# An audio tower's attention and expert block: another order of the work at the head

## What is computed

```python
logits = xn @ sn - sigmoid(gates)
q = einsum('tc,ecd,te->td', x, q_proj, m)      # k and v likewise
final = einsum('td,edc,te->tc', attn_out, o_proj, m * routing_weights)
```

## Time and profile before

| | |
|---|---|
| median of 3 runs | 722.53 us (721.84 to 722.65) |
| the profiled execution, its own time | 721.31 us |
| its span, first to last instruction | 719.6 us |
| TensorE busy (matmul) | 708.3 us, 98% |
| VectorE busy | 586.8 us, 82% |
| ScalarE busy | 371.9 us, 52% |
| GpSimd busy | 405.5 us, 56% |
| granted TensorE clock, mean | 1.000 |
| chain that ended last | 94% TensorE, 2% VectorE, 2% GpSimd |

### The profile page before, as it was taken

One profiled execution on the slowest core, in us unless ns is written; L12 is line 12 of the kernel. 1 busy time (PEld: TensorE's weight loads), 2 busy tenths in 40 slices (PEclk: granted clock), 3 DMA queues, 4 the chain that ended last, 5 costly groups with the idle time before them and its releaser, 6 DMA issues.

```text
span 719.6 us, 18107 instructions
## 1 busy us (share of the span) xinstructions
PE 708.3 (98%) x5384; PEld 467.0 (65%) x5384; DVE 586.8 (82%) x1474; ACT 371.9 (52%) x797; POOL 405.5 (56%) x657
## 2 busy tenths in 40 slices
PE   7999999999999999999999999999999999999996
PEld 6888666575756666575756666575756666575653
DVE  6788888888879888887979888887988898886626
ACT  3877463553646354553646354453646355463345
POOL 6542325746566575746566575746566574653344
PEclk9999999999999999999999999999999999999999
DMA  8681120202020110202020020202011020201000
GB/s 216 140 219 46 60 56 2 71 9 63 14 55 21 11 65 0 70 7 62 14 51 25 8 65 3 62 14 62 14 30 47 0 70 7 62 17 53 15 15 29
DMA packets 31216, 33.29 MB, mean 46 GB/s; under 512 B 5202, under 2 KB 27090, under 8 KB 31186
## 3 DMA queue, kind: packets, MB, share of 16 engines
q1 hardware_dynamic: 30114, 32.31, 16.9%
q10 hardware_dynamic: 1072, 0.60, 0.3%
HBM read 26.65 MB, written 6.25 MB: 46 GB/s over the span
## 4 chain that ended last, share of the span: by engine, by line
PE 94%; DVE 2%; POOL 2%; issue 1%; ACT 0%; POOLq 0%; DVEq 0%
PE bank L1520 75%; PE bank L1583 7%; PE bank L1442 4%; PE bank L1502 3%; PE bank L1654 1%; PE bank L1431 1%; PE bank L1569 1%; PE bank L1632 1%; PE bank L1447 1%; PE bank L1594 0%; DVE xm L1139 0%; PE bank L1605 0%; PE bank L1597 0%; POOL xhl L566 0%; POOL exp_hl L493 0%
## 5 line engine op out<-in xcount | busy, mean ns | idle before, releaser
L1520 PE MATMUL bank<-xm,w_qkv 128*128 128x374 f16 x2304 | 415.7, 322 | 0.0
L1520 PEld LDWEIGHTS bank<-xm,w_qkv 128*128 128x128 f16 x2304 | 220.7, 98 | 139.5 <-DVE xm L1139 0.3
L806 ACT ACTIVATE region_c<-bank,out_w 128x256 f32<-128x256 f32 x180 | 84.8, 471 | 164.9 <-PE bank L1520 164.9
L1139 DVE TENSOR_TENSOR xm<-xT,mask_all 128x1496 f16<-128x1496 f16 x128 | 151.0, 1184 | 1.4 <-ACT h L688 1.4
L1520 PE MATMUL bank<-w_o,aoT 128*128 128x512 f16 x540 | 145.7, 379 | 0.1
L1060 DVE SCALAR_TENSOR_TENSOR h<-bank,out_w,h 128x256 f32 (+1 forms) x180 | 86.2, 479 | 45.2 <-ACT region_c L806 40.1
L598 POOL TENSOR_TENSOR region_c<-region_c 128x512 f32<-128x512 f32 x47 | 77.6, 1652 | 27.7 <-ACT region_c L806 23.0
L613 POOL TENSOR_TENSOR exp_hl<-exp,exp_hl 128x128 f16<-128x128 f32 (+2 forms) x48 | 38.8, 809 | 75.5 <-ACT exp_hl L783 75.5
L1520 PEld LDWEIGHTS bank<-w_o,aoT 128*128 128x128 f16 x540 | 50.2, 98 | 38.2 <-DVE h L1060 0.7
L1039 DVE TENSOR_SCALAR region_b<-h,moments,small 128x256 f32 (+1 forms) x96 | 48.8, 553 | 5.7 <-POOL small L519 5.7
L604 POOL TENSOR_TENSOR h<-region_c,h 128x256 f32 (+1 forms) x47 | 42.0, 894 | 16.0 <-POOL region_c L601 11.4
(11 more groups left out here) (183 smaller groups left out, 1058.0 us busy)
## 6 DMA issues: line engine op xcount, KB each, us to landing
mask_all<-d_mask SPq DMA_DIRECT2D x32, 384.0 KB, 3.8
h<-in_x_dram SPq DMA_DIRECT2D x16, 256.0 KB, 5.7
out_dram<-h SPq DMA_DIRECT2D x32, 128.0 KB
rnorm_row<-d_rnorm SPq DMA_DIRECT2D x16, 192.0 KB, 3.6
h<-in_x_dram SPq DMA_DIRECT2D x16, 112.0 KB, 5.9
out_dram<-h SPq DMA_DIRECT2D x16, 112.0 KB
xm<-in_L_ffn_q_proj_dram SPq DMA_DIRECT2D x2, 512.0 KB, 9.0
region_c<-in_L_ffn_k_proj_dram SPq DMA_DIRECT2D x2, 512.0 KB, 7.3
```

The lines of the kernel that those rows point to most:

```text
L806: a.activation(prod[:, prod_buf(n, t), q, :], pair_bank(n, p)[:, C:2 * C], ACT.Copy, scale=weights_out(n)[:, t, 2 * q + 1:2 * q + 2]).then ...
L1139: v.tensor_tensor(xm[:, e, :, 0:T], xT[1][:, :, :, 0:T].rearrange("p a c t -> p (a c) t"), mask_all[:, e, 0:T].unsqueeze(1).broadcast_to([ ...
L1520: last = t_.matmul(dst, left[lp], right[rp], start=(starts and k == 0), stop=(stops and k == 2), skip_group_check=True)
```

## The change

The order of the head is changed on all engines, and no arithmetic:

- 38 warm-up matmuls instead of 46.
- SyncE loads weight piece 1 and the tiles of batch 7 ahead of the norm's round trip of batch 0.
- GpSimd sets `ones` ahead of `pick`.
- The bias has a semaphore of its own, so that TensorE's readout transposes no longer wait for it; these now come ahead of `turn_in(0)`, and the readout product ahead of `turn_in(1)`.
- ScalarE and VectorE round the token weights ahead of the first batch's split.
- The product with `ones` moves behind the whole projection of batch 0, and the wait for the last constant (`s_consts` 2) to `turn_first(0)`.
- `weights_high(0)` comes two batches earlier, `weights_high(1)` takes its place; `weights_low(1)` and `weights_low(2)` move earlier.
- The exponential's table is loaded by a dummy operation, and the gates' exponential comes behind those of batch 0's cosines.
- `route(0)` is no longer interrupted by `split_low(11)`, which precedes it.
- In the last batches of the head and in the branch `early(m)`: `mask_tokens(0, 1)` comes behind `split_low(15)` and `norm_apply(1, 1)`, `low_2(1)` ahead of `mask_tokens(0, 3)`, the wait for the last GELU ahead of the norm of batch 2, `weights_low(3)` behind `turned_low_2`; on TensorE the logits come one unit later, and the two halves of `turn_first` have a unit between them.

```diff
--- before.py
+++ after.py
@@ -178,6 +178,7 @@
         s_read_loaded = sem("read_loaded")
+        s_bias_loaded = sem("bias_loaded")
         s_consts = sem("consts")
@@ -296,7 +297,7 @@
         SPLIT = LAST // 16 * 16
-        WARM = 46
+        WARM = 38
         ENDS = (0, 1, 4, B)
@@ -418,11 +419,11 @@
             load_tiles(6)
+            load_weights(1)
+            load_tiles(7)
             norms_out(0)
             norms_in(0)
-            load_tiles(7)
             load_tiles(8)
-            load_weights(1)
             load_tiles(9)
@@ -474,6 +475,7 @@
             g.tensor_copy(ident16[:, :], ident[:, :]).then_inc(s_consts, 1)
+            g.memset(ones[:, :], 1.0)
             g.memset(pick32[:, :], 0.0).then_inc(s_picked, 1)
@@ -482,7 +484,6 @@
             g.tensor_copy(pick[:, :, :].rearrange("p b o -> p (b o)"), pick32[:, :]).then_inc(s_picked, 1)
-            g.memset(ones[:, :], 1.0)
             g.memset(p_half[:, :], 0.5)
@@ -662,7 +663,7 @@
             load_token_weights(1, s_tok_read)
-            act.dma_start(read_bias[:, :], tok_b.partition_broadcast(RR)).then_inc(s_read_loaded, 16)
+            act.dma_start(read_bias[:, :], tok_b.partition_broadcast(RR)).then_inc(s_bias_loaded, 16)
             for c in range(NC):
@@ -875,34 +876,35 @@
-            split_in(0)
             act.wait_ge(s_tok_loaded, 16)
             a.activation(w_tok[:, 0, :, :], stage_tok[:, 0, :, :], ACT.Copy, scale=W_SCALE).then_inc(s_tokw_hi, 1)
+            split_in(0)
             split_in(1)
...
             split_in(3)
+            weights_high(0)
             gelu(2)
...
             split_in(5)
-            weights_high(0)
+            weights_high(1)
             gelu(4)
...
             gelu(5)
-            act.wait_ge(s_small_loaded, 16 * (NC + 1))
-            a.activation(gate_tmp[:, 1, :], gate_tmp[:, 0, :], ACT.Exp, scale=-1.0).then_inc(s_gate_exp, 1)
+            a.activation(unused[:, :], log_p[:, :], ACT.Exp)
             exp_cosines(0, (0, 1))
...
             exp_cosines(0, (2,))
+            act.wait_ge(s_small_loaded, 16 * (NC + 1))
+            a.activation(gate_tmp[:, 1, :], gate_tmp[:, 0, :], ACT.Exp, scale=-1.0).then_inc(s_gate_exp, 1)
             gelu(6)
...
             a.activation(w_sim[:, :, 0, :], stage_sim[:, 3, :, :], ACT.Copy).then_inc(s_sim_hi, 1)
-            weights_high(1)
             gelu(7)
@@ -975,7 +977,7 @@
                 dve.wait_ge(s_setup_pe, 2)
-                dve.wait_ge(s_read_loaded, 32)
+                dve.wait_ge(s_bias_loaded, 16)
                 v.tensor_tensor(read_row[:, :], bank[4][0:RR, 0:C], read_bias[:, :], ALU.add).then_inc(s_setup_dve, 1)
@@ -1078,7 +1080,7 @@
-            def route(b, between=None):
+            def route(b):
@@ -1111,8 +1113,6 @@
                                       ALU.mult))
-                if between is not None:
-                    between()
                 v.tensor_scalar(row3[:, 1, :], row3[:, 0, :], 0.0, None, ALU.is_equal)
@@ -1252,13 +1252,12 @@
                 if early(m):
-                    mask_tokens(m, 3)
-                    low_2(f)
-                    for e in range(4, E):
+                    for e in range(3, E):
                         mask_tokens(m, e)
-                    weights_low(2 * NC - 1)
                     dve.wait_ge(s_xm_ready, E * f)
                     turned_low_2(f)
+                    weights_low(2 * NC - 1)
+                    dve.wait_ge(s_h_ready, B)
                     norm_stats(0, g1)
@@ -1355,8 +1354,8 @@
             read_columns()
+            token_weights_low()
             split_low(0)
-            token_weights_low()
             readout_row()
@@ -1374,6 +1373,7 @@
             split_low(6)
+            weights_low(1)
             cosines(0, 0)
@@ -1390,14 +1390,14 @@
             low_2(0)
-            weights_low(1)
             split_low(10)
             turned_low_2(0)
+            split_low(11)
             dve.wait_ge(s_consts, 2)
-            route(0, lambda: split_low(11))
+            route(0)
+            weights_low(2)
             weight_max(0)
             split_low(12)
-            weights_low(2)
             cosines(1, 0)
@@ -1410,11 +1410,11 @@
             mask_tokens(0, 0)
-            mask_tokens(0, 1)
             split_low(15)
             norm_apply(1, 1)
+            mask_tokens(0, 1)
             mask_tokens(0, 2)
-            dve.wait_ge(s_h_ready, B)
+            low_2(1)
             pipeline(dve, step)
@@ -1464,29 +1464,23 @@
                 t_.matmul(bank[6][:, 0:P], ident16[:, :], ident16[:, :], start=True, stop=True)
-            turn_in(0)
-
-            pe.wait_ge(s_read_loaded, 32)
+            pe.wait_ge(s_read_loaded, 16)
             pe.wait_ge(s_pad_zeroed, 2)
...
             last.then_inc(s_setup_pe, 1)
-            turn_in(1)
+            turn_in(0)
             pe.wait_ge(s_tok_read, 16)
...
             last.then_inc(s_setup_pe, 1)
+            turn_in(1)
             pe.wait_ge(s_tokw_lo, 1)
...
             project_tile(0, NT - 1)
-            pe.wait_ge(s_setup_dve, 3)
-            pe.wait_ge(s_consts, 2)
-            for c in range(NC):
-                last = t_.matmul(bank[5][:, 0:E], ones[:, :], stage_sim[:, 1, c, :], start=(c == 0), stop=(c == NC - 1))
-            last.then_inc(s_setup_pe, 1)
             pe.wait_ge(s_setup_dve, 6)
@@ -1494,6 +1488,9 @@
             add_row(0, NT - 1)
+            for c in range(NC):
+                last = t_.matmul(bank[5][:, 0:E], ones[:, :], stage_sim[:, 1, c, :], start=(c == 0), stop=(c == NC - 1))
+            last.then_inc(s_setup_pe, 1)
@@ -1503,15 +1500,23 @@
-            def turn_first(b):
+            def turn_first_high(b):
...
                 turn_rows(0, b, 0, turn[0], s_turned1_hi)
+
+            def turn_first_low(b):
+
                 pe.wait_ge(s_lo1, b + 1)
                 turn_rows(0, b, 1, turn[1], s_turned1_lo)
+
+            def turn_first(b):
+
+                turn_first_high(b)
+                turn_first_low(b)
@@ -1707,13 +1712,15 @@
                     turn_rows(1, f, 1, turn[1], s_turned2_lo)
-                    M(*range(2, 6))
+                    M(*range(2, 7))
                     logits(f)
-                    M(*range(6, 12))
+                    M(*range(7, 13))
                     turn_mask(f)
-                    M(*range(12, 22))
-                    turn_first(g1)
-                    M(22, 23)
+                    M(*range(13, 22))
+                    turn_first_high(g1)
+                    M(22)
+                    turn_first_low(g1)
+                    M(23)
                     return
@@ -1812,6 +1819,7 @@
             project(4)
+            pe.wait_ge(s_consts, 2)
             turn_first(0)
```

## The result

The changed kernel takes 718.67 us (median of six runs, 718.22 to 719.97) against 722.7 for the kernel before (six runs, 721.84 to 723.02) on the same chip: ratio 0.9948, 95% interval [0.9939, 0.9958]. It is faster, by 0.52%, and the forecast of 718.3 was 0.4 us too low. The profiled execution took 719.55, its span is 717.8.

What follows compares the result with a forecast made beforehand. TensorE was taken as the bound, always busy in the loop, so only its waits in the head could gain. The terms sum to 4.24 us, taking the median from 722.53 to 718.3 us, range 716.9 to 720.6.

Steps and rivals of the forecast that it cites:

- start: Opening of the head: pick product at 11.05 instead of 12.80, ones-product moved behind the batch: 1.47 us gained.
- piece 0 and the third GELU: Head, third GELU: ScalarE waits 0.6 for piece 0, first half ends 19.07, TensorE needs it at 19.03: -0.04 us.
- transposes behind routing: Head, transposes at 52.64: they no longer wait for a split placed in the middle of routing: 0.59 us.
- attention of batch 1: Head, at 62.54: 0.11 us kept of a possible 0.74, as piece 2's rounding slows GpSimd's mask steps.
- a split ahead of a mask product: Head, TensorE's gap at 71.04: moving a split ahead of one mask product gains 0.17 us.
- turned low rows of batch 1: Loop's first step: the gap from unit 1's end at 75.74 to the transposes at 75.98 goes, 0.24 us.
- first step's logits: Loop's first step: the gap from four units' end at 80.13 to the logits at 81.06 goes, 0.93 us.
- turned low rows of batch 2: End of the head: the wait from 97.06 to 97.54 goes, as a unit lies between the halves, 0.48 us.
- Rival (a): Head: GpSimd is not held up by piece 2's rounding, 0.63 us more gain, 717.6 us; chance 0.10.
- (c): Only the start's and the first step's gaps are real, new waits eat the rest: 721.1 to 724 us; chance 0.07.
- (d): Sync queue serves piece 0 with loads put behind it; it lands 6.0 late, holding the third GELU: 724.3 us; chance 0.03.
- (b): Head: piece 0 or the norm's round trip late, or the opening at 1.2 GHz: 719 to 721 us; chance 0.18.

Runs made afterwards that it cites:

- u1_split_between: Changed kernel with the split of batch 11 in the middle of routing again: 719.25 us, ratio 0.996 to the kernel before.
- u2_old_step: Changed kernel with VectorE's and TensorE's old order around the loop's first step: 719.5 us, ratio 0.9965 to the kernel before.
- u3_turn_joined: Changed kernel with both halves of batch 2's turned rows together, no unit between: 718.81 us, ratio 0.9958 to the kernel before.
- r1_after_again: The changed kernel run again, nothing edited: 717.66 us against 721.26 for the kernel before, ratio 0.9949.
- r2_row_first: Changed kernel with VectorE doing the readout row ahead of the square of the gate weights: 717.65 us, ratio 0.9949 to the kernel before.
- x1_pool_waits: r2_row_first, with GpSimd zeroing the two exponential tiles only after the readout row is split: 717.87 us, ratio 0.9932 to the kernel before.
- u5_ones_back: Changed kernel with the ones-product ahead of the pick product again, with its wait for GpSimd's constants: 720.58 us, ratio 0.997 to the kernel before.
- x2_piece_later: x1_pool_waits, with ScalarE's rounding of weight piece 0 behind the third GELU: 718.01 us, ratio 0.9935 to the kernel before.
- r3_max_later: Changed kernel with split_low(12) ahead of weight_max(0) on VectorE: 717.07 us, ratio 0.9943 to the kernel before.
- b2_all: x2_piece_later plus r3_max_later's edit and GpSimd's loop wait for the first mask product: 715.86 us, ratio 0.9907 to the kernel before.
- u4_warm_16: Changed kernel with 16 warm-up matmuls instead of 38: 718.41 us, ratio 0.9951 to the kernel before.

## Why the prediction was right, and where its steps were not

The sum was 4.24, the head gave 3.67 by the same steps. By these the profiled execution was to become 717.1; without long turns it took 717.65. That the median came within 0.4 of the forecast is luck in part: the medians differ by 4.03, more than the head's 3.66 can give, while where the kernel before is steady they differ by 3.60.

| step | forecast | measured | |
|---|---|---|---|
| start | 1.47 | 1.18 | mis-sized |
| piece 0 and the third GELU | -0.04 | 0 | right; ScalarE waits 0.28 and not 0.6, as the start gained 0.3 less |
| logits of batch 0 | 0.29 | 0.22 | nearly |
| transposes behind routing | 0.59 | 0.59 | right (u1_split_between: 0.71) |
| attention of batch 1 | 0.11 | 0.01 | size off, mechanism right |
| a split ahead of a mask product | 0.17 | 0 | wrong |
| turned low rows of batch 1 | 0.24 | 0.24 | right |
| first step's logits | 0.93 | 0.95 | right (with the row below, u2_old_step: 1.2) |
| turned low rows of batch 2 | 0.48 | 0.48 | right, half of it by the unit between (u3_turn_joined) |

**The start.** The step that was mis-sized is "then 0.1 and the old chain of 1.26 ... so 10.98". I took three durations of before as the operations' own. The second of them is a wait in disguise: it ends at 10.88 whether it begins at 10.51 (before), 10.29 (after), 10.02 (r1_after_again) or 8.36 (r2_row_first), because GpSimd's memsets of the exponential tiles hold it, and x1_pool_waits frees it (0.29). The chain could not move by 0.34 as I had it; it ended at 11.32 as before. The same sentence's other bound, a start at 8.4, would have given nothing either (r2_row_first). The whole 1.18 hangs on the move of the ones-product (u5_ones_back). Two slips of the sum are small: 1.31 and 0.17 make 1.48, and 9.60 + 0.1 + 1.26 makes 10.96.

**The clock.** I worked out a rise at 5.88 from one execution and called the case's own run evidence for the next. It rose between 6.6 and 7.8 in the two executions of the changed kernel, at about 5.0 in r2_row_first and x2_piece_later (the spacing of the warm-up falls from 0.107 to 0.056 there), near 8.1 in x1_pool_waits. The changed kernel paid nothing, since the hold on VectorE hid up to 1.18 us of it, but this was luck in my sum: without the hold the clock's moment is worth 0.78 of the start (x1_pool_waits against x2_piece_later). The Trainium skill (TensorE: Matmul & The Clock Gate, Part 1) says that the moment of the rise varies from run to run; the traces agree, with the same 38 matmuls in 4.24 and in 3.58 us.

**Rival (a)**, GpSimd not held by the rounding of piece 2, is refuted: its first mask step took 1.04. I had kept 0.11 of 0.74; 0.01 was had, and r3_max_later gets 0.62 of the rest back. Here I had read the hold in the earlier trace rows and used it. It is the same mechanism, seen from the other engine, that I missed at the start.

**The 0.17** was no gap of VectorE's making. In the changed kernel ScalarE's and TensorE's timelines have

```profile
68.48 0.60 ACT L686 ACTIVATE h<-bank 128x512 f32<-128x512 f32 x1 [1.04 <-PE bank L1447]
...
69.22 0.82 PE L1442 MATMUL bank<-w_tok,xinT 128*128 128x256 f16 x6
```

The projection starts 0.14 after the GELU's first part has read its bank (69.08), and before it was 0.14 too (70.47 + 0.60, then 71.21). VectorE's split, done at 70.93 before and at 68.10 after, shortens nothing there by being ready earlier. I had read the gap's length and not what ended it.

**"The loop hands on whatever shift it gets"** is true to 0.01 where the race goes the same way in every turn (the 13 turns behind the marker sum to 529.31 in r1_after_again and to 529.32 before) and is not a law: a turn in which a late mask lets GpSimd go first costs 0.55 to 0.76 more. Rivals (c) and (d) did not come about; the issue of piece 1 and of the tile load behind piece 0 did not delay it (9.3 again, and 8.8 to 9.5 in the other runs). Of (b) the low clock did come (the warm-up stood at it to its end), but the hold on VectorE hid it.

**The signs.** Two of the signs that I had named for being wrong appeared, though the forecast held: the warm-up spacing stayed at 0.107 to its end, and the shift shrank inside the loop. The first cost nothing, and the second was the race, so neither told what I had meant by it. Of the signs for being right, the marker stands at 97.07 and not near 96.5.

What stays open: I have one trace of the kernel before, and it has no long turn. That its medians of 722.4 and 722.46 in the later groups, against 721.26 in the first, come from such turns is argued only. Its times speak for it: the sixteen of the last group lie in four clusters (721.31 to 721.38, 721.82 to 721.96, 722.46 to 722.62, 723.01 to 723.26), 0.5 to 0.6 apart, about what one long turn costs. Whether zeroing on another engine than GpSimd would beat b2_all was not tried.

## What to carry to other kernels

- A duration read from a trace is not yet an operation's cost. Compare it with the same form elsewhere in the trace before it goes into a sum, and ask what the other engines ran beside it; an operation that always ends at the same moment is waiting.
- Work without a deadline (zeroing constants, a rounding that is needed later) can be on the critical path through a neighbour that it holds. One wait on a semaphore, which put it behind the urgent operation, was worth 0.26 to 1.04 us here at the pick product, by the clock's moment (on top of r2_row_first, which alone gave nothing).
- Where two engines race for the first start in each turn of a loop, fix the order by a wait. It cost nothing here in the turns that went well, and took the loss out of the others, not by ending the hold but by moving it to an operation that has time.

## What the runs showed of the hardware that I had not expected

- Some operations of VectorE and GpSimd hold each other, both ways, and the one that starts first keeps its speed. VectorE's scaling of a 48x256 tile: 0.28 to 0.29 alone, 2.52 beside the memsets. Its mask product: 0.97 first, 2.37 second. GpSimd's subtraction of the low rows: 1.61 first, 2.31 second; its mask step 1.04 beside a rounding of 1.22 and 0.24 without. VectorE's split, which reads PSUM (line 963), is not touched: it took 1.02 from 8.09, under the memsets of 7.27 to 10.61, and 1.02 from 7.89 in b2_all, where GpSimd was idle. The Trainium skill (GPSIMD Engine Reference, 1. Specifications) has the two sharing their SBUF interfaces, with contention for VectorE instructions in a 2-port mode or with two SBUF inputs. The traces agree as far as the operations named above go. In one point the Trainium skill and the measurement differ, and the measurement decides: not every instruction with two SBUF inputs is held. The low half of the token weights (line 953, from 7.02) ended at 7.70, in 0.68, in the middle of memsets that ran on to 10.61.
- Between two memsets VectorE did not get in: the held scaling of r2_row_first ran from 8.36, under the first of two memsets of 1.39 and 2.03 back to back, past the end of the second. That is no rule for every pair: in the long turn at 171 us the held mask product ended at 173.87, 0.8 behind the end of the subtraction (173.07), though GpSimd's next addition (line 599) had begun at 173.03; this time the addition was the one that stretched, to 1.96, where the same addition took 1.26 at 168.00 in r1_after_again.
- The granted clock reads 1.00 also where the spacing is that of 1.2 GHz. The windows of u4_warm_16 have, with the columns of the earlier trace rows,

```profile
8.00:12.00 4.00, 4.00 (x23) 2.87 (x22) 2.77 (x7) 0.98 (x2) 3.61 (x8) 1.00 0.94 264
```

  and until about 10.7 the matmuls of this stretch took twice their usual time. In these traces the spacing of equal matmuls is what tells the level.
